# Plain attention layer: tail values as 16 blocks, reciprocals moved behind the first main scores, three bank pairs for the maxima

## The chip, the cores and the metric

The kernel runs on one core of a Trainium2 chip. The metric is the device time of one execution in microseconds (us), lower is better. Three runs of the kernel before gave 2407.03 to 2410.1 us, median 2409.3 us. A core has TensorE (PE, matmuls; PEld its weight loads), VectorE (DVE), ScalarE (ACT), GpSimd (POOL) and SyncE (SP, here the queue that starts all DMA transfers). They run side by side and meet only at semaphores. SBUF is the memory on the core; PSUM is where TensorE writes, in banks of 128 x 512 floats.

## The reference

Two layers run one after the other on x, of shape 2 x 2048 x 512, with 154 context rows per batch:

```
for layer in (0, 1):
    x = x + tanh(g_xattn[layer]) * cross_attention(layernorm(x), ctx_1024)   # 16 heads of 32, 154 keys
    x = x + tanh(g_ffn[layer]) * ffn(layernorm(x))                           # 512 -> 2048 -> 512
```

Layer 0 (the plain layer) has no mask and no norm on q, k and v, and a relu in its ffn. Layer 1 normalises q, k and v, applies a mask, and rounds to a fixed-point grid around a piecewise gelu. Everything is float32.

## The kernel before

Both layers are built by one function, layer_phase, with the flag norm (False for the plain layer). The 4096 rows of x are taken in 8 chunks of 512 (it = 0 to 7). Attention runs over all chunks, then the ffn over all chunks. In the trace the attention of the plain layer takes the stretch from about 65 to 480 us; each chunk from 2 to 6 has the same pattern, about 51 us long. Names in the trace carry prefixes such as l_at_ and l_lay_.

The 16 heads stand in four groups (t = 0 to 3) of four (j = 0 to 3). The 154 keys are split: 128 are the main keys, 26 the tail keys. The tails of the four heads of a group lie in four slots of 32 partitions of p_tail[:, t, :], in the order that group_of(t, j) = (t + j) mod 4 gives. In float32 each matmul is recorded twice; a product of two rounded parts (hi, lo) is three matmuls.

PSUM is six banks named score (the last two of them are also values and sums) and two named bank. Within chunk `it`, TensorE does in this order (the kernel writes the order of every engine out by hand):

- xT_front and neg_front (L1406, L1502): transposes of the next chunk's rows and of the maxima; scores_tail (L1517), 16 blocks of 32 x 32, one for each head, that go to score banks 0 to 3; scores_tail_max (L1526).
- sums_front of the chunk before (L1590).
- q_front for chunk it+1 (L69), group by group, into bank[t % 2]; scores_main (L1546, L1549), which needs the score banks to have been read by the exponentials; values_of (L1563 the tail values, L1567 the main values, L1575 the sums, L1580 the tail sums, at t = 0 only).
- recips of the chunk before (L1609): transposes of the widened reciprocals into bank[0] and bank[1]; DVE multiplies the values by them (c_back, L1019) and ACT and DVE split the product (cT_back L742, lo_of L1036).
- 16 rounds of max_of for chunk it+1 (L1490), which take the pair of score banks 0,1 and 2,3 in turn (round m waits for the reduction of round m-2); from round 2 on a round is followed by three matmuls of y_back, the output projection of chunk it-1.

In the order before, the queue of TensorE in a chunk reads: q_front 0, scores 0, q_front 1, scores 1, values 0, q_front 2 and 3, scores 2, values 1, scores 3, recips 0 and 1, values 2, recips 2 and 3, maxima 0 and 1, values 3, the other maxima with y_back. The tail values are four matmuls with 128 rows and 32 columns (L1563) at the start of every values_of, accumulated in the bank values with the main ones. ACT moves the four results out of that bank (c_evict, L727).

DVE does, per chunk: the low parts of xT (L975), the reciprocals (L1042), q_low 0 and 1 (L983: q32 minus its rounded part, both in SBUF), norm_stats and norm_apply for a later chunk (L934, L943), q_low 2 and 3, c_back, and the 16 reductions (L1012). ACT fills q (q_fill L673), rounds it (q_hi_of L679) and takes the exponentials (L713 tail, L720 main). POOL widens the reciprocals (widen, L543) and adds the gated bias to the residual rows, four rows of 512 per partition in one instruction (add_bias, L534), when the transfer of those rows has landed.

The wait that the change touches most is that of q_front: before, for t >= 2, it is

```
pe.wait_ge(q_row if norm else q_filled, KT * it + t - 1)
if norm and it >= 2:
    pe.wait_ge(c_normed, KT * (it - 2) + t - 1)
```

Of the kernel before, what the change touches and what calls it, by code (L numbers as in the profile page):

```python
# [191 lines left out]
def layer_phase(nc, pre, w, ident, ident_bf, gates, gate, gate_f, norm, place, x_in, front, ahead, src,  # L192
                mid, dst):

    with ExitStack() as ctx:
# [109 lines left out]
        seeded = n.sem("seeded")  # L305
        dve_seeded, act_seeded = n.sem("dve_seeded"), n.sem("act_seeded")
# [304 lines left out]
        def _(act):  # L611
# [110 lines left out]

            def c_evict(it, t):
# [94 lines left out]
            for it in range(NCH):  # L818
                more = it < last
                xT_front(it + 1, (0, 1))  # L820
                neg_front(it)
                xT_front(it + 1, (2, 3))
                exps_tail(it)
                if norm:
                    seed_main(it, 0)
                if it < B:
                    v_tail_of(it)
                if not norm:
                    if more:
                        q_front(it + 1, (0,))  # L830
                    else:
                        relu_hi(0)
                exps_main(it, 0)
                if norm:
                    seed_main(it, 1)
                if not norm:
                    if more:
                        q_front(it + 1, (1,))
                    else:
                        relu_hi(1)  # L840
                exps_main(it, 1)
                if norm:
                    seed_main(it, 2)
                c_evict(it, 0)
                if more and not norm:
                    q_front(it + 1, (2, 3))
                exps_main(it, 2)
                if norm:
                    seed_main(it, 3)
                c_evict(it, 1)  # L850
                if it and norm:
                    cT_back(it - 1, (0, 1))
                exps_main(it, 3)
                if it and not norm:
                    cT_back(it - 1, (0, 1))
                elif not it:
                    front.round_hi(act, "wd")
                c_evict(it, 2)
# [6 lines left out]
                c_evict(it, 3)  # L865
# [63 lines left out]
        def _(dve):  # L929
# [77 lines left out]
            def max_of(it, m):  # L1007
                t, q = m // QT, m % QT
                dve.wait_ge(max_ps, NM * it + m + 1)
                heads = max_banks(it if norm else 0, m).rearrange("p a (h k) -> p a h k", h=2)  # L1010
                to = maxes[:, q, :].rearrange("p (j c) -> p j c", c=DH)[:, :, t]
                nc.vector.tensor_reduce(to, heads, AX.X, ALU.max).then_inc(max_done, 1)  # L1012

            def c_back(it, ts):
                for t in ts:
                    u = KT * it + t
                    c = c_sb[:, it % 2, t, :]
                    dve.wait_ge(rT_ps, u + 1)
                    nc.vector.tensor_tensor(c, c, bank[t % 2][:, :], ALU.mult).then_inc(c_normed, 1)  # L1019
                    if t != ts[0]:  # L1020
                        lo_of(it, t - 1)
                lo_of(it, ts[-1])

            def c_mult(it, ts):
                for t in ts:
                    c = c_sb[:, it % 2, t, :]
                    dve.wait_ge(rT_ps, KT * it + t + 1)
                    nc.vector.tensor_tensor(c, c, bank[t % 2][:, :], ALU.mult).then_inc(c_normed, 1)
# [197 lines left out]
            for it in range(last):  # L1226
# [21 lines left out]
                else:  # L1248
                    q_low(it + 1, (0, 1))
                    norm_stats(it + 2)  # L1250
                    q_low(it + 1, (2, 3))
                    norm_apply(it + 2)
                if it and norm:
                    c_mult(it - 1, (2, 3))
                    c_low(it - 1, (0, 1))
                elif it:
                    c_back(it - 1, (0, 1))
                if norm:
                    norm_apply(it + 2)
                if it and norm:  # L1260
# [20 lines left out]
            for u in range(2):  # L1281
# [3 lines left out]
                else:  # L1285
                    relu_lo(u)
# [7 lines left out]
            else:  # L1294
                c_back(last - 1, (0, 1))
                c_back(last - 1, (2, 3))
            y_back(last - 1, 0)
# [82 lines left out]
        def _(pe):  # L1380
# [56 lines left out]
            def q_front(it, ts):  # L1437
# [30 lines left out]
            def max_of(it, m):  # L1468
# [16 lines left out]
                for a in range(2):  # L1485
                    to = max_banks(it if norm else 0, m)[:, a, :].rearrange("p (h k) -> p h k", h=2)
# [42 lines left out]
            def scores_main(it, t):  # L1529
# [7 lines left out]
                for i, (a, c) in enumerate(((0, 0), (0, 1), (1, 0))):  # L1537
                    for j in range(GH):
                        if i == 0:
                            if not norm:  # L1540
# [10 lines left out]

            def values_of(it, t):
# [6 lines left out]
                if t == 0 and it % CPB == 0:  # L1559
                    pe.wait_ge(v_placed, V_COPIES * (b + 1))  # L1560
                for j in range(GH):
                    own = slice(DH * j, DH * (j + 1))
                    nc.tensor.matmul(values[own, :], keys.v_tail[:, b, t, own], p_tail[:, t, :],  # L1563
                                     start=True, stop=False, skip_group_check=True)
                for j in range(GH):
# [3 lines left out]
                                            p_main[:, t % 2, j, :], start=False, stop=True,  # L1569
# [25 lines left out]
            def recips(it, ts):  # L1595
                for t in ts:
# [5 lines left out]
                    elif t < 2 and it + 2 < NCH:  # L1602
                        pe.wait_ge(q_filled, KT * (it + 2) + t + 3)
                    elif t < 2:
                        pe.wait_ge(y_done, QT * (it - 1) + 3 + t)
                    else:
                        pe.wait_ge(c_normed, KT * it + t - 1)
                    for q in range(QT):
# [81 lines left out]
            for it in range(NCH):  # L1690
# [13 lines left out]
                scores_main(it, 0)  # L1704
                if more:
                    q_front(it + 1, (1,))
                else:
                    first_product(1)
                scores_main(it, 1)
# [3 lines left out]
                if more:  # L1713
                    q_front(it + 1, (2, 3))
                scores_main(it, 2)
                values_of(it, 1)
# [3 lines left out]
                if it and not norm:  # L1720
                    recips(it - 1, (0, 1))
# [144 lines left out]
```

## Time and profile before

| | |
|---|---|
| median of three runs | 2409.3 us |
| profiled execution, its own time | 2409.38 us |
| its span | 2407.6 us |
| TensorE busy | 2352.2 us, 98% |
| VectorE busy | 1504.9 us, 63% |
| ScalarE busy | 1181.1 us, 49% |
| GpSimd busy | 238.6 us, 10% |
| mean granted TensorE clock | 0.991 |

The span is the time from the first to the last recorded instruction; 1.8 us lie around it. Matmuls are pipelined: a matmul of 0.39 us is followed by the next after 0.23 us, so that what a group of matmuls costs is read from the start of one group to the start of the next, not from its duration. Similarly on DVE and ACT the next instruction starts a little before the end of the one before it is recorded.

### The profile page before, as it was taken

What the parts mean: (1) busy time and instruction counts of PE and PEld (TensorE: products, weight loads), DVE (VectorE), ACT (ScalarE), POOL (GpSimd) and SP (SyncE); (2) the same over time, 40 slices, a digit from 0 to 9 for tenths busy, and PEclk for the clock granted to TensorE, in tenths of its full rate; (3) what the DMA queues carried; (4) which work ended last, traced back from release to release, by engine and by line L of the source; (5) the groups of instructions that cost most, each with busy time, mean ns of one, the idle gap of its engine ahead of it and who ended that gap; (6) DMA issues with size and microseconds to landing.
All of it is one profiled execution on the core that took longest, in us unless ns stands there. A gap on an engine that the chain in (4) does not pass through costs nothing.

```text
span 2407.6 us, 32695 instructions
## 1 busy us (share of the span) xinstructions
PE 2352.2 (98%) x12984; PEld 1793.4 (74%) x12984; DVE 1504.9 (63%) x2467; ACT 1181.1 (49%) x1912; POOL 238.6 (10%) x219
## 2 busy tenths in 40 slices
PE   7999999999999999999988999999999999999998
PEld 5566666688888888888765666666788888888886
DVE  5566666442222222223488888886988987988986
ACT  4554434442222222223335666666666666666665
POOL 1021112210000000000111111113000000000000
PEclk9999999999999999999998999999999999999999
DMA  3121112421101101102311111224301001110000
GB/s 130 36 88 53 53 54 80 161 80 53 50 4 53 53 1 53 53 3 86 121 64 50 67 68 67 67 71 145 105 29 43 36 36 36 36 38 33 36 35 19
DMA packets 89159, 140.95 MB, mean 59 GB/s; under 512 B 5040, under 2 KB 27952, under 8 KB 89008
## 3 DMA queue, kind: packets, MB, share of 16 engines
q1 hardware_dynamic: 89008, 138.87, 16.9%
q8 instruction: 103, 1.69, 0.3%
q14 instruction: 48, 0.39, 0.1%
HBM read 105.30 MB, written 33.55 MB: 58 GB/s over the span
## 4 chain that ended last, share of the span: by engine, by line
PE 39%; DVE 8%; ACT 2%; issue 2%; POOL 0%; DVEq 0%; ACTq 0%
PE l_lay_bank L69 19%; PE l_lay_score L69 11%; PE l_lay_score L1490 1%; PE l_lay_score L1546 1%; PE l_lay_score L1563 1%; DVE l_at_at_next L1089 1%; PE l_lay_score L1575 1%; PE l_lay_score L1567 1%; DVE l_at_h_lo L1103 1%; DVE l_at_at_next L1082 1%; PE l_lay_bank L1406 1%; DVE l_at_full L1078 1%; DVE l_at_full L1071 1%; DVE l_at_xTf_lo L975 1%; DVE l_at_maxes L1012 1%
## 5 line engine op out<-in xcount | busy, mean ns | idle before, releaser
L69 PE MATMUL l_lay_score<-l_at_tw_hi,l_at_h_hi 128*128 128x512 f32 x1024 | 401.5, 392 | 5.4 <-DVE l_at_h_lo L1103 4.8
L69 PE MATMUL l_lay_bank<-l_at_xTf_hi,l_at_tw_hi 128*128 128x512 f32 x1024 | 400.0, 391 | 0.0
L69 PE MATMUL l_lay_score<-l_at_tw_hi,l_at_h_lo 128*128 128x512 f32 x1024 | 398.8, 389 | 0.0
L69 PE MATMUL l_lay_bank<-l_at_xTf_hi,l_at_tw_lo 128*128 128x512 f32 x1024 | 398.4, 389 | 0.0
L69 PE MATMUL l_lay_bank<-l_at_xTf_lo,l_at_tw_hi 128*128 128x512 f32 x1024 | 398.4, 389 | 0.0
L69 PE MATMUL l_lay_score<-l_at_tw_lo,l_at_h_hi 128*128 128x512 f32 x1024 | 398.4, 389 | 0.0
L1063 DVE TENSOR_TENSOR l_at_h_lo<-l_at_full,l_at_h_hi 128x512 fp32r<-128x512 f32 x128 | 93.4, 729 | 468.5 <-ACT l_at_h_hi L760 468.5
L755 ACT ACTIVATE l_at_full<-l_lay_bank,l_at_lay_b 128x512 f32<-128x512 f32 x128 | 88.5, 691 | 456.6 <-PE l_lay_bank L69 456.6
L69 PEld LDWEIGHTS l_lay_score<-l_at_tw_hi,l_at_h_hi 128*128 128x128 f32 x1024 | 192.2, 188 | 49.3 <-DVE l_at_h_lo L1103 10.4
L69 PEld LDWEIGHTS l_lay_score<-l_at_tw_hi,l_at_h_lo 128*128 128x128 f32 x1024 | 192.2, 188 | 40.3
L69 PEld LDWEIGHTS l_lay_bank<-l_at_xTf_hi,l_at_tw_hi 128*128 128x128 f32 x1024 | 192.3, 188 | 40.1 <-issue 0.7
L69 PEld LDWEIGHTS l_lay_bank<-l_at_xTf_hi,l_at_tw_lo 128*128 128x128 f32 x1024 | 192.2, 188 | 40.0
L69 PEld LDWEIGHTS l_lay_bank<-l_at_xTf_lo,l_at_tw_hi 128*128 128x128 f32 x1024 | 192.3, 188 | 39.3
L69 PEld LDWEIGHTS l_lay_score<-l_at_tw_lo,l_at_h_hi 128*128 128x128 f32 x1024 | 192.3, 188 | 39.0
L1012 DVE TENSOR_REDUCE l_at_maxes<-l_lay_score 128x4 f32<-128x616 f32 x256 | 197.4, 797 | 27.2 <-PE l_lay_score L1490 24.5
L720 ACT ACTIVATE l_at_p_main<-l_lay_score 128x512 f32<-128x512 f32 x256 | 131.9, 602 | 106.0 <-PE l_lay_score L1549 106.0
L781 ACT ACTIVATE l_at_at_grid<-l_at_at_grid,l_at_lay_grid_bias 128x512 f32<-128x512 f32 x128 | 92.9, 726 | 149.3 <-DVE l_at_at_grid L1093 149.3
L1490 PE MATMUL l_lay_score<-l_at_k_bd,l_at_qT_hi 128*128 128x308 f32 x512 | 130.4, 340 | 6.9 <-ACT l_lay_score L693 3.3
L767 ACT ACTIVATE l_at_grid<-l_at_full,l_at_lay_grid_bias 128x512 f32<-128x512 f32 x128 | 92.4, 722 | 89.5 <-DVE l_at_full L1071 89.5
L1103 DVE SCALAR_TENSOR_TENSOR l_at_h_lo<-l_at_at_grid,l_at_h_hi 128x512 fp32r<-128x512 f32 x128 | 88.1, 688 | 58.2 <-ACT l_at_h_hi L786 58.2
L667 ACT ACTIVATE l_at_xT_hi<-l_lay_bank 128x512 fp32r<-128x512 f32 x64 | 36.6, 597 | 174.7 <-PE l_lay_bank L1406 174.7
L1490 PEld LDWEIGHTS l_lay_score<-l_at_k_bd,l_at_qT_hi 128*128 128x128 f32 x512 | 94.6, 196 | 36.9 <-DVE l_at_maxes L1012 10.0
(196 smaller groups left out, 4063.0 us busy)
## 6 DMA issues: line engine op xcount, KB each, us to landing
both_x_in<-stream SPq DMA_DIRECT2D x25, 1024.0 KB, 5.6
l_at_xg<-stream SPq DMA_DIRECT2D x23, 1024.0 KB, 5.5
stream<-l_at_xg SPq DMA_DIRECT2D x22, 1024.0 KB, 4.3
l_at_tw_raw<-in_l_w SPq DMA_DIRECT2D x64, 256.0 KB, 5.5
both_x_in<-in_x SPq DMA_DIRECT2D x9, 1024.0 KB, 7.8
l_at_xg<-in_x SPq DMA_DIRECT2D x7, 1024.0 KB, 5.5
out<-l_at_xg SPq DMA_DIRECT2D x7, 1024.0 KB, 4.3
l_at_maskT_in<-in_maskT SPq DMA_DIRECT2D x16, 256.0 KB, 3.5
```

The lines of the kernel that those rows point to most:

```text
L69: done = nc.tensor.matmul(out, lhs[a], rhs[b], start=first and n == 0, stop=last and n == len(passes) - 1)
L667: nc.scalar.activation((xT if i < NCH else xTf)[0][:, k, :], (bank if i <= NCH else tr)[k % 2][:, :], ACT.Copy)\
L720: nc.scalar.activation(p_main[:, t % 2, j, :], score[:, j, :], ACT.Exp)\
L755: nc.scalar.activation(full[u % 2][:, :], hid[u % 2][:, :], ACT.Relu, bias=b1[:, u % MT:u % MT + 1]).then_inc(h_full, 1)
L767: nc.scalar.activation(grid[u % 2][:, :], full[u % 2][:, :], ACT.Identity, bias=grid_bias[:, 2:3]).then_inc(gridded, 1)
L781: nc.scalar.activation(at_grid[u % AB][:, :], at_grid[u % AB][:, :], ACT.Identity, bias=grid_bias[:, 3:4]).then_inc(rounded, 1)
L975: nc.vector.tensor_tensor(to[1][:, k, :], ps[k % 2][:, :], to[0][:, k, :].bitcast(F32), ALU.subtract)\
L1012: nc.vector.tensor_reduce(to, heads, AX.X, ALU.max).then_inc(max_done, 1)
L1063: nc.vector.tensor_tensor(h[1][u % HB][:, :], full[u % 2][:, :], h[0][u % HB][:, :].bitcast(F32), ALU.subtract)\
L1071: nc.vector.tensor_scalar(full[u % 2][:, :], hid[u % 2][:, :], b1[:, u % MT:u % MT + 1], ROUND_IN, ALU.add, ALU.add)\
L1103: nc.vector.scalar_tensor_tensor(h[1][u % HB][:, :], at_grid[u % AB][:, :], -ROUND_256, h[0][u % HB][:, :].bitcast(F32), ALU.add, ALU.subt ...
L1490: done = nc.tensor.matmul(to, qT_of(it)[0][:, t, q * P:(q + 1) * P], keys.bd[:, b, t, 2 * a:2 * a + 2, :], start=not norm, stop=True, skip ...
```

## The change

Only the plain layer's order changes, but for one wait that both layers share. Cut to its core:

```diff
@@ TensorE
+            def tail_values(it):
+                pe.wait_ge(exp_done, NS * it + KT)
+                ...
+                for t in range(KT):
+                    for j in range(GH):
+                        c = own_rows[group_of(t, j)]
+                        to = score[own_rows[j], t, :] if t else values[own_rows[j], :]
+                        done = nc.tensor.matmul(to, keys.v_tail[c, b, t, own_rows[j]], p_tail[c, t, :],
+                                                start=True, stop=t > 0, skip_group_check=True)
+                    if t:
+                        done.then_inc(tail_v_ps, 1)
@@ q_front, t >= 2
-                        if norm and it >= 2:
+                        if it >= 2:
                             pe.wait_ge(c_normed, KT * (it - 2) + t - 1)
@@ max_of
+                elif it and m == SEED0:
+                    pe.wait_ge(c_out, KT * it)
+                    pe.wait_ge(s_out, it)
+                elif it and m > SEED0:
+                    pe.wait_ge(max_done, NM * it + pair_before(m) + 1)
-                    to = max_banks(it if norm else 0, m)[:, a, :].rearrange("p (h k) -> p h k", h=2)
+                    to = max_banks(it, m)[:, a, :].rearrange("p (h k) -> p h k", h=2)
@@ scores_main, first pass
-                            if not norm:
+                            if not norm and t == 0 and j == 1:
+                                pe.wait_ge(tail_v_dve, it + 1)
+                            elif not norm and t == 0 and j > 1:
+                                pe.wait_ge(tail_v_act, 2 * it + j - 1)
+                            elif not norm:
@@ y_back
+                if i < KT:
+                    pe.wait_ge(cT_lo, KT * it + i + 1)
                 if i == 0:
-                    pe.wait_ge(cT_lo, KT * it + KT)
+                    pe.wait_ge(c_normed, KT * it + KT)
@@ TensorE, order in a chunk
-                scores_main(it, 0)
+                tail_values(it)
                 q_front(it + 1, (1,))
+                scores_main(it, 0)
+                if it:
+                    recips(it - 1, (0, 1))
+                if more:
+                    q_front(it + 1, (2,))
                 scores_main(it, 1)
                 values_of(it, 0)
-                q_front(it + 1, (2, 3))
                 scores_main(it, 2)
+                q_front(it + 1, (3,))
-                values_of(it, 1)
                 scores_main(it, 3)
-                recips(it - 1, (0, 1))
+                values_of(it, 1)
                 values_of(it, 2)
@@ ACT: two of the tail values are moved to c_sb; only result 0 is evicted
+                    tail_values_out(it, 2)
+                    tail_values_out(it, 3)
@@ DVE
+                    tail_values_out(it, 1)
                     q_low(it + 1, (0, 1))
+                    if it:
+                        c_mult(it - 1, (0, 1))
                     norm_stats(it + 2)
-                    q_low(it + 1, (2, 3))
+                    q_low(it + 1, (2,))
                     norm_apply(it + 2)
+                    q_low(it + 1, (3,))
+                    c_add(it, 1)
                 elif it:
-                    c_back(it - 1, (0, 1))
+                    c_low(it - 1, (0, 1))
+                    c_add(it, 2)
-                    c_back(it - 1, (2, 3))
+                    c_mult(it - 1, (2, 3))
                 for m in range(NM):
                     max_of(it + 1, m)
+                    if m < 2 and it and not norm:
+                        c_low(it - 1, (m + 2,))
+                    if m == 2 and not norm:
+                        c_add(it, 3)
@@ new on DVE
+            def c_add(it, t):
+                c = c_sb[:, it % 2, t, :]
+                if t == 1:
+                    dve.wait_ge(tail_v_dve, it + 1)
+                else:
+                    dve.wait_ge(tail_v_act, 2 * it + t - 1)
+                dve.wait_ge(c_ps, KT * it + t + 1)
+                nc.vector.tensor_tensor(c, values, c, ALU.add).then_inc(c_out, 1)
```

So the tail values of group 0 stay in the bank values and are accumulated with the main ones as before; those of groups 1 to 3 go to score banks 1 to 3, are copied to c_sb, and DVE adds the main values to them later. c_mult is the multiplication of c_back alone, c_low its splitting alone. In rounds 4 to 15 the maxima use a third pair, the banks values and sums. In the last chunk the queue of TensorE has first_product 0 and 1 where the others have q_front 0 and 1, and no q_front 2 and 3.

## Rows read from the trace of the kernel before

**Rows 1.** The page: busy time, and the span in 40 slices of 60.2 us.
```profile
PE 2352.2 (98%) x12984; PEld 1793.4 (74%) x12984; DVE 1504.9 (63%) x2467; ACT 1181.1 (49%) x1912; POOL 238.6 (10%) x219
PE   7999999999999999999988999999999999999998
```

**Rows 2.** Waits of PE from 95 to 480 us: total, times, longest.
```profile
PE l_lay_score L1490 <- DVE l_at_maxes L1012: 2.3, 8, 0.7
PE l_lay_score L1563 <- ACT l_at_c_sb L727: 1.1, 1, 1.1
```

**Rows 3.** Timeline of PE, chunk 5: start us, us, engine, line, instruction, count.
```profile
317.57 1.14 PE L1517 MATMUL l_lay_score<-l_at_q,l_at_k_tail 32*32 32x512 f32 x32
318.64 1.09 PE L1406 MATMUL l_lay_bank<-ident,both_x_in 128*128 128x128 f32 x8
...
321.31 0.50 PE L69 MATMUL l_lay_bank<-l_at_xT_hi,l_front_wq_hi 128*128 128x512 f32 x1
...
324.25 0.50 PE L1546 MATMUL l_lay_score<-l_at_qT_hi,l_at_k_hi 32*128 32x512 f32 x4
...
325.38 0.50 PE L69 MATMUL l_lay_bank<-l_at_xT_hi,l_front_wq_hi 128*128 128x512 f32 x1
...
329.48 1.06 PE L1563 MATMUL l_lay_score<-l_at_p_tail,l_at_v_tail 128*32 128x512 f32 x8
330.36 1.04 PE L1567 MATMUL l_lay_score<-l_at_p_main,l_at_v_main 128*32 128x512 f32 x8
331.22 1.04 PE L1575 MATMUL l_lay_score<-l_at_p_main,l_at_e_main 128*32 128x512 f32 x8
```

**Rows 4.** The same from 347 to 354 us: recips, then two rounds of maxima.
```profile
347.42 1.09 PE L1609 MATMUL l_lay_bank<-ident,l_at_r_wide 128*128 128x128 f32 x8
348.27 0.80 PE L1490 MATMUL l_lay_score<-l_at_k_bd,l_at_qT_hi 128*128 128x308 f32 x4
...
352.80 0.45 PE L1490 MATMUL l_lay_score<-l_at_k_bd,l_at_qT_hi 128*128 128x308 f32 x2
...
353.78 0.45 PE L1490 MATMUL l_lay_score<-l_at_k_bd,l_at_qT_hi 128*128 128x308 f32 x2
```

**Rows 5.** Timeline of DVE, chunk 5: q_low 0 and 1; a c_mult pair of chunk 4.
```profile
325.84 0.69 DVE L983 TENSOR_TENSOR l_at_qT_lo<-l_at_q,l_at_qT_hi 128x512 fp32r<-128x512 f32 x1 [3.79 <-ACT l_at_qT_hi L679]
329.94 1.62 DVE L983 TENSOR_TENSOR l_at_qT_lo<-l_at_q,l_at_qT_hi 128x512 fp32r<-128x512 f32 x1 [3.40 <-ACT l_at_qT_hi L679]
...
293.37 1.28 DVE L1019 TENSOR_TENSOR l_at_c_sb<-l_at_c_sb,l_lay_bank 128x512 f32<-128x512 f32 x2 [1.57 <-PE l_lay_bank L1609]
```

**Rows 6.** Timeline of POOL in the same chunk: add_bias.
```profile
326.33 4.68 POOL L534 TENSOR_TENSOR l_at_xg<-l_at_xg,l_at_gate_bias 128x2048 f32<-128x2048 f32 x1 [3.04 <-DMA l_at_xg<-in_x]
```

**Rows 7.** Chunk 1: q_low 1 on DVE, add_bias on POOL.
```profile
125.84 4.34 DVE L983 TENSOR_TENSOR l_at_qT_lo<-l_at_q,l_at_qT_hi 128x512 fp32r<-128x512 f32 x1 [3.40 <-ACT l_at_qT_hi L679]
125.05 4.58 POOL L534 TENSOR_TENSOR l_at_xg<-l_at_xg,l_at_gate_bias 128x2048 f32<-128x2048 f32 x1 [5.86 <-DMA l_at_xg<-in_x]
```

**Rows 8.** Groups of DVE from 0 to 480 us: busy us, mean ns, idle before.
```profile
L983 DVE TENSOR_TENSOR l_at_qT_lo<-l_at_q,l_at_qT_hi 128x512 fp32r<-128x512 f32 x32 | 33.9, 1059 | 95.6 <-ACT l_at_qT_hi L679 95.6
```

**Rows 9.** Chunk 0: values 3 on PE, the later maxima on PE and DVE.
```profile
97.55 1.06 PE L1563 MATMUL l_lay_score<-l_at_p_tail,l_at_v_tail 128*32 128x512 f32 x8 [1.12 <-ACT l_at_c_sb L727]
100.27 0.84 PE L1490 MATMUL l_lay_score<-l_at_k_bd,l_at_qT_hi 128*128 128x308 f32 x4
100.86 10.67 DVE L1012 TENSOR_REDUCE l_at_maxes<-l_lay_score 128x4 f32<-128x616 f32 x14 [3.15 <-PE l_lay_score L1490]
```

**Rows 10.** Layer 1: two idle stretches of PE before q_front.
```profile
1316.77 0.47 PE L69 MATMUL l_lay_bank<-l_front_wq_hi,l_at_xT_hi 128*128 128x512 f32 x1 [2.30 <-DVE l_at_c_sb L1028]
1538.87 0.47 PE L69 MATMUL l_lay_bank<-l_front_wq_hi,l_at_xT_hi 128*128 128x512 f32 x1 [1.23 <-DVE l_at_c_sb L1028]
```

**Rows 11.** Stretches: length, busy us of PE, PEld, DVE, ACT, POOL, clock, DMA.
```profile
1315.00:1319.00 4.00, 2.23 (x7) 1.84 (x8) 4.00 (x8) 0.00 (x0) 0.76 (x2) 0.83 0.72 209
1319.00:1323.00 4.00, 4.00 (x14) 3.17 (x14) 3.92 (x12) 0.00 (x0) 1.03 (x2) 0.74 0.02 5
```

More of the change, by code:

```diff
@@ L305, in layer_phase @@
         seeded = n.sem("seeded")
+        tail_v_ps, tail_v_dve, tail_v_act = (n.sem(s) for s in ("tail_v_ps", "tail_v_dve", "tail_v_act"))
         dve_seeded, act_seeded = n.sem("dve_seeded"), n.sem("act_seeded")
@@ L721, in exps_main, with tail_values_out @@
                         .then_inc(exp_done, 1)
+            def tail_values_out(it, t):
+                act.wait_ge(tail_v_ps, 3 * it + t)
+                if it >= 2:
+                    act.wait_ge(cT_lo, KT * (it - 2) + t + 1)
+                nc.scalar.activation(c_sb[:, it % 2, t, :], score[:, t, :], ACT.Copy).then_inc(tail_v_act, 1)
             def c_evict(it, t):
@@ L840, in _ @@
                         relu_hi(1)
+                exps_main(it, 0)
+                if norm:
+                    seed_main(it, 1)
+                if more and not norm:
+                    q_front(it + 1, (2,))
                 exps_main(it, 1)
@@ L1017, in c_back @@
                     c = c_sb[:, it % 2, t, :]
+                    if not norm:
+                        dve.wait_ge(c_out, u + 1)
                     dve.wait_ge(rT_ps, u + 1)
@@ L1026, in c_mult @@
                     c = c_sb[:, it % 2, t, :]
+                    if not norm:
+                        dve.wait_ge(c_out, KT * it + t + 1)
                     dve.wait_ge(rT_ps, KT * it + t + 1)
@@ L1284, in _ @@
                     round_hidden(u)
-                else:
-                    relu_lo(u)
+            if not norm:
+                tail_values_out(last, 1)
+                relu_lo(0)
+                relu_lo(1)
+                c_add(last, 1)
             if norm:
@@ L1295, in _ @@
                 c_back(last - 1, (0, 1))
+                c_add(last, 2)
                 c_back(last - 1, (2, 3))
+                c_add(last, 3)
             y_back(last - 1, 0)
@@ L1558, in values_of @@
                     pe.wait_ge(kv_bias, 8)
[L1559 to L1564, printed above, removed]
+                if norm:
+                    if t == 0 and it % CPB == 0:
+                        pe.wait_ge(v_placed, V_COPIES * (b + 1))
+                    for j in range(GH):
+                        own = slice(DH * j, DH * (j + 1))
+                        nc.tensor.matmul(values[own, :], keys.v_tail[:, b, t, own], p_tail[:, t, :],
+                                         start=True, stop=False, skip_group_check=True)
                 for j in range(GH):
@@ L1568, in values_of @@
                                             keys.v_main[:, b, DH * head:DH * (head + 1)],
-                                            p_main[:, t % 2, j, :], start=False, stop=True,
+                                            p_main[:, t % 2, j, :], start=t > 0 and not norm, stop=True,
                                             skip_group_check=True)
@@ L1607, in recips @@
                         pe.wait_ge(c_normed, KT * it + t - 1)
+                        if not norm and it + 2 < NCH:
+                            pe.wait_ge(q_filled, KT * (it + 2) + t + 1)
                     for q in range(QT):
@@ L1708, in _ @@
                     first_product(1)
+                if not norm:
+                    scores_main(it, 0)
+                    if it:
+                        recips(it - 1, (0, 1))
+                    if more:
+                        q_front(it + 1, (2,))
                 scores_main(it, 1)
@@ L1712, in _ @@
                 values_of(it, 0)
-                if more:
+                if more and norm:
                     q_front(it + 1, (2, 3))
                 scores_main(it, 2)
-                values_of(it, 1)
+                if more and not norm:
+                    q_front(it + 1, (3,))
+                else:
+                    values_of(it, 1)
                 if norm and it:
@@ L1719, in _ @@
                 scores_main(it, 3)
-                if it and not norm:
-                    recips(it - 1, (0, 1))
+                if more and not norm:
+                    values_of(it, 1)
                 values_of(it, 2)
```

39 lines of the change are left out of this document (25 added, 14 removed).

## The prediction

> **What bounds the kernel now.** I read the page first, for the shares of the engines and the slices: TensorE is 98% busy, and in the slices of the plain layer's attention (the second to the eighth) it stands at 9 [rows 1]. Then the waits of TensorE for that stretch: from 95 to 480 us it waited 4.1 us in all, of which 2.3 for the reductions of the maxima and 1.1, once, for an eviction [rows 2]. So this stretch is bound by TensorE's own queue: what is taken from that queue is won, and each new wait in it is lost in full, since nothing idle stands behind it. Then I read the timeline of one chunk on each engine (chunk 5, from 315.92 us to 366.93 us, 51.0 us), because the change reorders a chunk, and asked at every step of the new order which wait ends last.
>
> **What the queue of TensorE gains.** The tail values cost 329.48 to 330.36, 0.88 us, four times a chunk: 3.52 us [rows 3]. In their place come 16 blocks of 32 x 32. The nearest row is scores_tail, 16 blocks of the same shape: 317.57 to 318.64, 1.07 us. That gives 2.45 us a chunk. The changes between groups of different shape cost some 0.1 us each; one fewer is left (values 1 and 2 now follow each other) and one more is made (q_front 2 and 3 are parted), and recips followed by q_front cost 0.85 as before maxima [rows 4], not the 1.02 that I read before values. All starts added up, a chunk would take 48.5 us if nothing waited: 2.5 us won.
>
> The price of the 16 blocks is bounded so: below by one pass of 0.86 us as the main values take [rows 3]; above by four passes one after the other, 3.44 us. I take 1.07, as the row of the same shape has it. Trainium skill, "TensorEngine Tiling (Array Packing)", Gotcha 1: PSUM Pressure, says that different row tiles can't use one PSUM bank at the same time. The new blocks do that (the four blocks of a group come from four row tiles and go to one bank). The blocks of scores_tail do it too, and by 1.07 us for all 16 the trace doesn't agree. By that rule it would be the upper bound.
>
> **What it loses, first place: q_front 2 behind c_mult 0.** Now recips 0 and 1 stand before q_front 2 and use the same bank, so q_front 2 waits (c_normed) until DVE has done c_mult 0. On DVE c_mult 0 stands behind q_low 1, and that waits for ACT to fill and round q 1. Let E be the start of scores 0 before (324.25 in chunk 5). TensorE is ready for q_front 2 at E + 1.07 (tail) + 2.94 (q_front 1, as 321.31 to 324.25) + 1.13 (scores, 324.25 to 325.38) + 0.85 = E + 6.0 [rows 3, 4]. DVE starts q_low 1.59 us after the end of a q_front (324.25 to 325.84 [rows 3, 5]), so q_low 1 at E + 5.6; at 0.65 us until the next instruction may start, and 0.64 to 0.68 for c_mult (1.28 for two), c_mult 0 ends at E + 6.93 and TensorE goes on at about E + 6.97. That is 0.95 us of waiting, in chunks 1 to 6: 5.7 us.
>
> But q_low 1 doesn't take 0.69 us here. In chunk 5 it took 1.62 and ended 0.55 us after add_bias on POOL (331.56 against 326.33 + 4.68 = 331.01) [rows 5, 6]; in chunk 1 4.34, again 0.55 us after POOL (130.18 against 129.63) [rows 7]. The group says how much that is over the layer: 32 instructions at 0.69 would be 22.1 us, and they took 33.9 [rows 8]; 11.8 us too many, and by the timelines they lie in six q_low 1, of chunks 1 to 6 (4.34, 2.97, 2.87, 2.23, 1.62 and 1.81 us). Before, norm_stats stood behind q_low 1 and nobody waited for it. Now c_mult 0 does, and TensorE for that. q_low 1 keeps its place (E + 5.6 against E + 5.69 before), and so does add_bias: it starts when its transfer lands, and this hangs on the end of the output projection a chunk earlier, whose distance to the chunk's start is left as it is. So the 11.7 us go into TensorE's wait, with 6 x 0.09 for the earlier start: 5.7 + 11.7 + 0.5 = 17.9 us, from 4.7 us in chunk 1 to 1.9 in chunk 5. If POOL's instruction slid out of the way it would be 5.7; if it slid a us later, 24. I take 17.9. Trainium skill, "SBUF — State Buffer", section SBUF: two separate sides, says that DVE with two SBUF inputs and GpSimd share a port pair as an exclusive lock for the whole instruction. The rows agree: 1.62 and 4.34 against 0.69 us. c_mult has one of its inputs in PSUM, and by that rule runs free; it is what I assumed.
>
> **Second place: maxima round 4.** It writes the banks values and sums, so it waits for c_add 3. DVE does, from the end of c_mult 3 on: maxima 0, c_low 2, maxima 1, c_low 3, maxima 2, c_add 3. At 0.76 us for a reduction (10.67 / 14 [rows 9]) and 0.65 for the others that is 4.2 us. Counted on from recips 2, c_add 3 ends 0.77 us after TensorE is ready for round 4. With 0.12 us before values 2 (c_add 1, behind q_low 3) it is 0.9 us a chunk, 5.3 us for six. After that a round with its y_back takes TensorE 0.98 us [rows 4] and DVE 0.76 plus three y_back: the third pair brings nothing there, and DVE is not the bound. Between 0 and 1.5 us a chunk is possible; I take 0.9.
>
> The other new waits end early: tail values out on ACT (0.62 us each) are done about 1.2 us before scores 0; exponentials 3, now behind values 1 in the queue, end 0.5 us before maxima 0; the widening on POOL is done some 6 us ahead. If one of these covers went, it would cost its difference alone.
>
> **Chunk 0** has no recips, so not the first wait. The wait of 1.12 us before values 3 goes (c_add 2 isn't behind the rounding of wd), and the tail gain comes: round 2 of the maxima starts at about 97.1 instead of 100.27 [rows 9]. From there DVE is the bound, 14 reductions in 10.67 us, and c_add 3 is added (0.65): 3.1 - 0.65 = 2.5 us won. A third bank pair helps nothing where DVE has no gap. **Chunk 7** has no q_front 2, so scores 1 comes right behind recips and waits for exponentials 0, some 1.4 us; 2.5 - 1.4 = 1.1 us won. The wait of y_back on cT_lo, now split, was no wait before in either layer: nothing, and the rest of layer 1 keeps its order.
>
> **Sum without the clock.** Chunks 1 to 6: 6 x 2.5 = 15.0 won, 17.9 + 5.3 = 23.2 lost: 8.2 us slower. Chunks 0 and 7: 3.6 us faster. Together 4.6 us slower, 2414.0 against the profiled execution's 2409.38, which lies 0.1 us above the median.
>
> **The clock.** After 2.30 us idle before 1316.77 the granted clock went to 0.83 and 0.74 over the next two stretches of 4 us [rows 10, 11], which is a while at 1.2 instead of 2.4 GHz: 0.17 x 4 + 0.26 x 4 = 1.7 us lost. After 1.23 us idle before 1538.87 it stayed at 1.00 in the windows there. The new waits are 4.7, 3.3, 3.2, 2.5, 1.9 and 2.1 us in chunks 1 to 6. I count a fall for the four that are longer than 2.30: 4 x 1.7 = 6.8 us, bounds 0 and 6 x 1.7 = 10.2. That makes 2420.7; for the part of a fall that lies inside the idle time I take off 1: 2419.7.
>
> **The rivals.**
> A. *The long wait doesn't come*: POOL's add_bias moves off, or q_low 1 gets in before it. For it: the landing times of the transfer varied by some 1.5 us between the chunks. Against: all six were hit before, and POOL's 4.6 us cover E + 5.6 in each. Then 5.7 instead of 17.9 and no clock loss: 2409.4 - 15.0 - 3.6 + 5.7 + 5.3 = 2401.8. This is the case on the other side: TensorE's 2.5 us a chunk decide as soon as the new waits stay under them. Chance 0.14.
> B. *The wait comes, the clock stays*: the idle stretches fall so that the clock isn't taken back. For it: 1.23 us left it alone. Against: 2.30 didn't. 2414. Chance 0.22.
> C. *The 16 blocks are done in four passes*, by the page's rule: 2.4 us more a chunk. Part of it hides in the first wait, which then ends at the same time: about 19 us more, less 11 hidden: some 2422 with B's clock, as there the waits are short. Against it stands scores_tail. Chance 0.05.
> D. My forecast: the wait and the clock, 2419.7. Chance 0.59.
>
> **How the numbers follow.** From no change a measurement of this kernel can tell about 0.2%, 4.8 us. A is faster. B at 2414 lies on the edge of 0.2% (2414.1) and goes half to same, half to slower; of D a tenth may end within 0.2%, if two falls alone come. Faster 0.13, same 0.17, slower 0.70. The range reaches from 2404, which leaves out A's lower part, to 2428, which takes in 24 us instead of 17.9 and two more falls; without A the range would be 2411 to 2428.
>
> **What would show it.** In the profile after: L1517's and the new tail group's starts 1.07 us apart from the next group; q_front (L69) idle before it, released by DVE's c_mult, 1.9 to 4.7 us in six chunks, with q_low 1 still at 1.6 to 4.4 us; maxima (L1490) waiting 0.8 us for DVE at round 4; a clock below 1.00 in the slices from 110 to 400 us; chunks of 51.3 us and more. I am wrong if q_front's wait is about 1 us or names another engine, if a chunk takes under 51 us, or if the tail group takes over 3 us.

## The result, and the profile after

The changed kernel takes 2416.66 us (median of eight runs, 2415.03 to 2420.12), the kernel before 2409.45 us beside it (eight runs, 2403.57 to 2411.72). The ratio is 1.0035, 95% interval 1.0026 to 1.0044: slower by 7.2 us or 0.35%. The forecast was 2419.7 us. The profiled execution took 2417.11 us, 7.7 us more than that of before.

The page of the changed kernel first: TensorE's busy time has fallen by 9.3 us and the span has grown by 7.7, so its idle time has grown by 17.0 us. The busy time is not all work: it holds what the falls of the clock below add to the matmuls.

```profile
span 2415.3 us, 32800 instructions
PE 2342.9 (97%) x12984; PEld 1789.8 (74%) x12984; DVE 1521.0 (63%) x2499; ACT 1174.5 (49%) x1904; POOL 240.3 (10%) x219
```

The waits of TensorE from 60 to 490 us (total, times, longest). The first three are new beside [rows 2]. In the first, by far the largest, q_front waits for c_mult; in the other two round 4 of the maxima waits (the third row is chunk 0, where it waits for c_add 3).

```profile
PE l_lay_bank L69 <- DVE l_at_c_sb L1057: 15.9, 6, 4.3
PE l_lay_score L1540 <- issue: 2.5, 6, 0.4
PE l_lay_score L1540 <- DVE l_at_c_sb L1037: 1.3, 1, 1.3
PE l_lay_score L1540 <- DVE l_at_maxes L1022: 1.2, 6, 0.3
```

The timeline of TensorE shows where: the first matmul of q_front 2 in chunks 1 to 6.

```profile
128.83 0.77 PE L69 MATMUL l_lay_bank<-l_at_xT_hi,l_front_wq_hi 128*128 128x512 f32 x1 [4.31 <-DVE l_at_c_sb L1057]
...
183.99 0.47 PE L69 MATMUL l_lay_bank<-l_at_xT_hi,l_front_wq_hi 128*128 128x512 f32 x1 [3.32 <-DVE l_at_c_sb L1057]
...
237.29 0.47 PE L69 MATMUL l_lay_bank<-l_at_xT_hi,l_front_wq_hi 128*128 128x512 f32 x1 [1.98 <-DVE l_at_c_sb L1057]
...
289.18 0.47 PE L69 MATMUL l_lay_bank<-l_at_xT_hi,l_front_wq_hi 128*128 128x512 f32 x1 [2.16 <-DVE l_at_c_sb L1057]
...
342.47 0.47 PE L69 MATMUL l_lay_bank<-l_at_xT_hi,l_front_wq_hi 128*128 128x512 f32 x1 [1.99 <-DVE l_at_c_sb L1057]
...
394.33 0.47 PE L69 MATMUL l_lay_bank<-l_at_xT_hi,l_front_wq_hi 128*128 128x512 f32 x1 [2.13 <-DVE l_at_c_sb L1057]
```

What DVE and POOL did in chunk 5 answers to [rows 5, 6]: q_low 1 takes 1.88 us and ends 0.54 us after add_bias (341.72 against 341.18), and c_mult stands right behind it.

```profile
339.84 1.88 DVE L993 TENSOR_TENSOR l_at_qT_lo<-l_at_q,l_at_qT_hi 128x512 fp32r<-128x512 f32 x1 [3.11 <-ACT l_at_qT_hi L680]
341.65 1.27 DVE L1057 TENSOR_TENSOR l_at_c_sb<-l_at_c_sb,l_lay_bank 128x512 f32<-128x512 f32 x2
...
336.31 4.87 POOL L535 TENSOR_TENSOR l_at_xg<-l_at_xg,l_at_gate_bias 128x2048 f32<-128x2048 f32 x1 [3.07 <-DMA l_at_xg<-in_x]
```

The granted clock around six of these waits (columns as in [rows 11]; the clock stands behind POOL's column):

```profile
126.00:130.00 4.00, 1.17 (x3) 1.01 (x4) 4.00 (x5) 0.00 (x0) 1.53 (x1) 0.56 0.00 0
130.00:134.00 4.00, 4.00 (x15) 2.87 (x17) 2.04 (x8) 0.06 (x1) 1.76 (x4) 0.58 0.00 0
184.00:188.00 4.00, 4.00 (x11) 3.17 (x12) 3.20 (x10) 0.00 (x0) 0.60 (x2) 0.57 0.00 0
...
236.00:240.00 4.00, 2.71 (x12) 2.17 (x12) 4.00 (x7) 0.58 (x2) 0.00 (x0) 1.00 0.00 0
...
290.00:294.00 4.00, 4.00 (x18) 2.68 (x20) 2.39 (x9) 0.30 (x1) 1.41 (x3) 0.57 0.00 0
342.00:346.00 4.00, 3.53 (x24) 2.70 (x28) 3.68 (x11) 0.49 (x1) 0.20 (x1) 1.00 0.00 0
394.00:398.00 4.00, 3.67 (x24) 2.86 (x28) 3.54 (x11) 0.65 (x1) 0.26 (x2) 1.00 0.00 0
```

The clock was at 1.2 GHz for a while behind the waits of 4.31, 3.32 and 2.16 us (in the first it fell before the wait was over) and stayed at 2.4 GHz behind 1.98, 1.99 and 2.13 us.

From one start of neg_front to the next, the chunks took, in us:

```
chunk        0      1      2      3      4      5      6      sum
before   46.04  51.67  51.04  51.03  51.02  51.01  51.05   352.86
after    43.08  57.81  54.63  51.74  53.42  51.76  51.84   364.28
change   -2.96  +6.14  +3.59  +0.71  +2.40  +0.75  +0.79   +11.42
```

From chunk 7's neg_front on, the execution is 3.8 us shorter (1985.4 against 1989.2 us). Of this, 0.5 lie in chunk 7, the remainder behind it, where the two programs are nearly alike.

### The profile page after: what moved, and what is told of

Read it like the earlier page. It is cut to its first block, busy times and chain, and to the rows that moved or that the text cites. A ratio compares the mean times of both kernels' runs of the same rounds, so it can differ in the third digit from the quotient of the medians.

```text
span 2415.3 us, 32800 instructions
## 1 busy us (share of the span) xinstructions
PE 2342.9 (97%) x12984; PEld 1789.8 (74%) x12984; DVE 1521.0 (63%) x2499; ACT 1174.5 (49%) x1904; POOL 240.3 (10%) x219
## 4 chain that ended last, share of the span: by engine, by line
PE 38%; DVE 8%; ACT 2%; issue 2%; POOL 0%; DVEq 0%; ACTq 0%
PE l_lay_bank L69 19%; PE l_lay_score L69 11%; PE l_lay_score L1540 1%; PE l_lay_score L1600 1%; PE l_lay_score L1636 1%; DVE l_at_at_next L1118 1%; PE l_lay_score L1648 1%; PE l_lay_score L1640 1%; DVE l_at_h_lo L1132 1%; DVE l_at_at_next L1111 1%; DVE l_at_full L1107 1%; DVE l_at_full L1100 1%; PE l_lay_bank L1451 1%; DVE l_at_xTf_lo L985 1%; DVE l_at_maxes L1022 1%
## 5 line engine op out<-in xcount | busy, mean ns | idle before, releaser
L1540 PEld LDWEIGHTS l_lay_score<-l_at_k_bd,l_at_qT_hi 128*128 128x128 f32 x512 | 93.3, 194 | 41.1 <-issue 11.5
```

The costliest lines, as they stand in the source:

```text
L1540: done = nc.tensor.matmul(to, qT_of(it)[0][:, t, q * P:(q + 1) * P], keys.bd[:, b, t, 2 * a:2 * a + 2, :], start=not norm, stop=True, skip ...
```

## The experiments

Each is an edit of the changed kernel and was timed in five rounds beside the kernel before. All medians:

```
kernel               median us (lowest to highest, runs)   before    ratio [95% interval]
the change           2416.66 (2415.03 to 2420.12, 8)       2409.45   1.0035 [1.0026, 1.0044]
e1_mult_first        2401.21 (2398.69 to 2402.51, 6)       2408.73   0.9965 [0.9953, 0.9977]
e3_short_bias        2403.55 (2399.45 to 2404.37, 8)       2408.73   0.9978 [0.9968, 0.9988]
e4_recips_back       2402.35 (2399.13 to 2404.93, 6)       2408.73   0.9973 [0.9962, 0.9985]
e5_two_pairs         2415.13 (2410.01 to 2418.39, 7)       2408.73   1.0026 [1.0015, 1.0037]
e2_mult_add          2396.81 (2394.34 to 2401.54, 6)       2409.09   0.9955 [0.9941, 0.9968]
e6_late_recips       2393.94 (2392.64 to 2395.64, 5)       2409.09   0.9941 [0.9929, 0.9952]
e7_filled_wait       2414.69 (2412.97 to 2416.16, 8)       2409.09   1.0025 [1.0015, 1.0035]
```

The theory: q_front 2 waits for c_mult 0, which is late because q_low 1 stands ahead of it and is held by add_bias; the clock's falls come on top. The rivals: that the 16 blocks or the other moved steps cost the time, that the place of recips is at fault whatever DVE's order is, and that the clock is the larger part.

### e1_mult_first: c_mult ahead of q_low 1

```diff
-                    q_low(it + 1, (0, 1))
+                    q_low(it + 1, (0,))
                     if it:
                         c_mult(it - 1, (0, 1))
+                    q_low(it + 1, (1,))
```

> The changed kernel with one edit on DVE: c_mult 0 and 1 stand ahead of q_low 1 instead of behind it. My theory (q_front 2 waits for c_mult 0, and that for q_low 1, which POOL's add_bias stretches): the wait before q_front 2 falls from 15.9 us in six chunks to about 0.5 us each, 3 in all, the three falls of the clock go too (some 4 us), and the time is near 2416.7 - 13 - 4 = 2400. Rival 1 (the loss is in what the blocks and the shape changes cost TensorE, or in DVE's added work as such): DVE does the same work in another order, so nothing over 2 us moves, 2415 to 2417. Rival 2 (c_mult itself is stretched by POOL, or waits for the transposes): the wait keeps most of its length, 2412 to 2416.

2401.21 us. One instruction moved on DVE turns 0.35% slower into 0.35% faster. The waits of TensorE:

```profile
PE l_lay_bank L69 <- DVE l_at_c_sb L1057: 3.0, 6, 0.5
PE l_lay_score L1541 <- issue: 2.4, 6, 0.4
PE l_lay_score L1541 <- DVE l_at_c_sb L1037: 1.3, 1, 1.3
```

q_front 2 waits 3.0 us in all instead of 15.9, and chunks 2 to 6 take 50.2 to 50.3 us (but 51.7 in chunk 1). In chunk 5, c_mult starts while POOL is at add_bias, and q_low 1 comes when that is over and takes 0.68 us:

```profile
324.76 1.28 DVE L1057 TENSOR_TENSOR l_at_c_sb<-l_at_c_sb,l_lay_bank 128x512 f32<-128x512 f32 x2 [3.42 <-PE l_lay_bank L1685]
325.96 0.68 DVE L993 TENSOR_TENSOR l_at_qT_lo<-l_at_q,l_at_qT_hi 128x512 fp32r<-128x512 f32 x1
...
321.13 4.66 POOL L535 TENSOR_TENSOR l_at_xg<-l_at_xg,l_at_gate_bias 128x2048 f32<-128x2048 f32 x1 [3.25 <-DMA l_at_xg<-in_x]
```

c_mult takes its usual 0.64 us each: one of its inputs lies in PSUM, and it isn't held. In chunk 1 both lie wholly inside add_bias (123.76 to 125.04 us, against 122.54 to 127.13) and take 1.28 us together as well. The forecast had assumed this, and the rule of the Trainium skill, "SBUF — State Buffer", section SBUF: two separate sides, which names two SBUF inputs, agrees with it. The 16 blocks and the place of recips are unchanged here, so they are not what made the change slow.

### e3_short_bias: POOL's instruction shortened

The kernel leaves out most of the output bias of the plain layer.

```diff
+                if not norm and i < last:
+                    nc.gpsimd.tensor_tensor(to[:, 0, 0:8], to[:, 0, 0:8], rows[:, 0:8], ALU.add)\
+                        .then_inc(xg_done, 1)
+                    return
```

> The changed kernel, but POOL's add_bias in the plain layer's attention, for chunks 0 to 6, adds only 8 columns of one row in place of 4 x 512 (most of the output bias is left out). My theory: q_low 1 falls from 1.9 to 4.2 us to 0.69 in all chunks, and the wait before q_front 2 to about 0.95 us each, 5.7 in all: 10 us less, and with the falls of the clock 2416.7 - 10 - 4 = 2402 to 2404. Rival (q_low 1 is long for another reason, such as the timing of ACT's rounding or a transfer into SBUF): q_low 1 and the wait stay, 2415 to 2417.

2403.55 us. Groups of DVE from 0 to 480 us (busy us, mean ns, idle before), the changed kernel and then this one:

```profile
L993 DVE TENSOR_TENSOR l_at_qT_lo<-l_at_q,l_at_qT_hi 128x512 fp32r<-128x512 f32 x32 | 33.2, 1037 | 84.6 <-ACT l_at_qT_hi L680 84.6
```

```profile
L997 DVE TENSOR_TENSOR l_at_qT_lo<-l_at_q,l_at_qT_hi 128x512 fp32r<-128x512 f32 x32 | 22.1, 690 | 75.3 <-ACT l_at_qT_hi L684 75.3
```

All 32 q_low now take 0.68 to 0.69 us, and nothing on DVE was changed. The wait of q_front 2 in this kernel:

```profile
PE l_lay_bank L69 <- DVE l_at_c_sb L1061: 4.8, 6, 0.8
```

So 11.1 of the 15.9 us were POOL's instruction, as the excess of the group over 22.1 us (33.2 less 22.1 = 11.1) says by itself; the other 4.8 us, 0.8 a chunk, are the order on DVE.

### e4_recips_back: reciprocals 0 and 1 behind scores 3 again

The waits of the old order come back with it: q_front 2 of the plain layer no longer waits for c_normed, recips 0 and 1 wait until ACT has filled q 2 and 3, and in chunk 7 ACT does its part of splitting products 0 and 1 behind the last exponentials.

```diff
@@ TensorE
                     scores_main(it, 0)
-                    if it:
-                        recips(it - 1, (0, 1))
...
                 scores_main(it, 3)
+                if it and not norm:
+                    recips(it - 1, (0, 1))
                 if more and not norm:
                     values_of(it, 1)
@@ DVE
-                    if it:
-                        c_mult(it - 1, (0, 1))
...
                     q_low(it + 1, (3,))
+                    if it:
+                        c_mult(it - 1, (0, 1))
```

> The changed kernel with one part undone: recips 0 and 1 go back behind scores 3 (now ahead of values 1), DVE's c_mult 0 and 1 behind q_low 3, q_front 2 has no wait on c_normed in the plain layer; the 16 blocks and the three bank pairs stay. My theory: no wait of q_front; what is left per chunk is TensorE's own queue, 2.5 us shorter than before, less 0.4 at round 4 of the maxima: 2409.4 - 6 x 2.0 - 4 = 2393 to 2396. Rival 1 (the 16 blocks bring less than they seem to): 2405 to 2410. Rival 2 (the values' sum on DVE holds up values 2 or the maxima when c_mult stands beside it): 2398 to 2404, with waits of L1640 or L1540 for L1037.

2402.35 us, above what was expected. The wait of q_front is gone and chunks 2 to 6 take 49.7 to 49.8 us. Two terms had been set too low. The maxima's round 4 still waits for c_add 3 (below). And from chunk 7's neg_front to the chunk's own recips 1 it took 45.15 us, against 42.29 before and 41.85 in e1. With no recips behind scores 0, TensorE idles 1.11 us before the exponentials of group 0 are done, and then works at 1.2 GHz for a while: the granted clock was 0.83 in the 10 us from 420 on. Values 3 of that chunk also wait 0.6 us for c_add 2. The timeline of TensorE, then that stretch:

```profile
420.02 1.87 PE L1602 MATMUL l_lay_score<-l_at_qT_hi,l_at_k_hi 32*128 32x512 f32 x4 [1.11 <-ACT l_at_p_main L721]
```

```profile
420.00:430.00 10.00, 9.98 (x75) 3.49 (x75) 2.46 (x2) 5.89 (x12) 6.17 (x2) 0.83 0.01 2
```

### e5_two_pairs: the maxima back on two bank pairs

```diff
-                elif it and m == SEED0:
-                    pe.wait_ge(c_out, KT * it)
-                    pe.wait_ge(s_out, it)
-                elif it and m > SEED0:
-                    pe.wait_ge(max_done, NM * it + pair_before(m) + 1)
...
-                    to = max_banks(it, m)[:, a, :].rearrange("p (h k) -> p h k", h=2)
+                    to = max_banks(it if norm else 0, m)[:, a, :].rearrange("p (h k) -> p h k", h=2)
```

> The changed kernel with one part undone: the maxima of the plain layer take two bank pairs in turn in all rounds. My theory (the third pair brings nothing where TensorE is the bound, and costs the wait of round 4 for c_add 3): the waits of 0.4 us before round 4 in six chunks and 1.25 in chunk 0 go, 2416.7 - 2.5 - 0 to 1 = 2413 to 2415. Rival (the third pair decouples TensorE from DVE, which has more to do in these rounds now): waits of L1540 for L1022 appear in rounds 3 to 6, and the time is 2418 to 2422.

2415.13 us, 1.5 below the change; the intervals overlap, so the sign isn't sure. The trace shows two parts that nearly cancel. In chunk 5 of the changed kernel the rounds 3 and 4 start 1.55 us apart where the period is 0.98:

```profile
362.89 0.45 PE L1540 MATMUL l_lay_score<-l_at_k_bd,l_at_qT_hi 128*128 128x308 f32 x2
...
364.44 0.52 PE L1540 MATMUL l_lay_score<-l_at_k_bd,l_at_qT_hi 128*128 128x308 f32 x2 [0.40 <-issue]
```

With two pairs the same two rounds start 1.00 us apart, and the rounds 4 and 5 1.21 us, for the reduction behind c_add 3. So of the 0.57 us before round 4 some 0.2 come back a round later, and chunk 5 takes 51.39 us against 51.76:

```profile
362.79 0.45 PE L1535 MATMUL l_lay_score<-l_at_k_bd,l_at_qT_hi 128*128 128x308 f32 x2
363.79 0.52 PE L1535 MATMUL l_lay_score<-l_at_k_bd,l_at_qT_hi 128*128 128x308 f32 x2
365.00 0.55 PE L1535 MATMUL l_lay_score<-l_at_k_bd,l_at_qT_hi 128*128 128x308 f32 x2
```

In chunk 0, where DVE bounds the maxima, the third pair did help: neg_front of chunk 1 starts at 108.70 in the changed kernel and at 110.21 here. The wait on c_add 3 is the third pair's price, and the forecast's sentence that the pair helps nothing in chunk 0 was wrong. The 1.5 us are not the pair's alone, though: here the clock was at 0.50 in most of these rounds (0.73 from 102 to 104 us, 0.50 from 104 to 110), in the changed kernel from 106 us on. With three pairs such a clock cost nothing: in e1, at 0.50 from 102 to 110 us, chunk 0 took 43.11 us, the same as at full clock in e7. With the clock full for most of these rounds the pair is worth some 0.6 us: the 14 reductions from round 2 on took DVE 10.67 us before [rows 9], and 10.63 us with c_add 3 among them in the changed kernel (98.01 to 108.64).

### e2_mult_add: e1, and c_add 3 two places earlier

```diff
-                    if m < 2 and it and not norm:
-                        c_low(it - 1, (m + 2,))
-                    if m == 2 and not norm:
+                    if m in (0, 2) and it and not norm:
+                        c_low(it - 1, (2 + m // 2,))
+                    if m == 1 and not norm:
                         c_add(it, 3)
```

> e1_mult_first with one more edit on DVE: c_add 3 stands behind reduction 1 of the maxima instead of 2, and c_low 3 behind reduction 2. My theory (round 4 of the maxima waits for c_add 3, at 0.6 us a chunk as the starts of rounds 4 and 5 show, 1.3 in chunk 0): the gap between the starts of rounds 3 and 4 falls from 1.55 to 1.0 us, 4 us less in all, 2396 to 2398. Rival (round 4 waits for something else, as the profile puts it down to no releaser): 1.55 us stays, 2400 to 2402.

2396.81 us, 12.3 below its own runs of the kernel before, where e1 was 7.5 below its own: 4.8 us more. The chunk goes from 50.25 to 49.6 us; chunks 1 to 6 save 3.4 us together and chunk 0 another 0.6. The wait under "issue" that stood before round 4 is gone:

```profile
PE l_lay_bank L69 <- DVE l_at_c_sb L1057: 3.0, 6, 0.5
PE l_lay_score L1541 <- DVE l_at_maxes L1022: 1.4, 8, 0.2
```

### e6_late_recips: both waits removed

e4 in chunks 1 to 6, the changed kernel's order in chunk 7, and e2's order of c_add 3.

```diff
@@ TensorE
-                    if it:
+                    if not more:
                         recips(it - 1, (0, 1))
...
                 scores_main(it, 3)
+                if it and more and not norm:
+                    recips(it - 1, (0, 1))
```

> e4_recips_back, but in chunk 7 recips 0 and 1 stand right behind scores 0 as in the changed kernel, and c_add 3 stands behind reduction 1 as in e2_mult_add. In e4 a chunk took 49.8 us against 51.0 before, but chunk 7 took 2.9 us more than before, with a wait of 1.1 us for the exponentials and a fall of the clock. My theory: that was chunk 7's own wait; now a chunk takes 49.2 us, chunk 7 about what it took in e1_mult_first, and the time is 2393 to 2396. Rival (late recips cost by themselves, c_mult beside c_add holds up values 2): 2398 to 2402.

2393.94 us, ratio 0.9941: by the medians 15.2 us faster than the kernel before and 22.7 faster than the change. It beats both. All waits of TensorE from 60 to 490 us:

```profile
PE l_lay_score L1540 <- DVE l_at_maxes L1022: 0.7, 4, 0.2
PE l_lay_bank L69 <- DVE l_at_xT_lo L985: 0.6, 1, 0.6
PE l_lay_bank L1684 <- DVE l_at_xg L1081: 0.5, 1, 0.5
PE l_lay_score L1552 <- DVE l_at_maxes L1022: 0.4, 1, 0.4
PE l_lay_score L1540 <- ACT l_at_p_main L721: 0.2, 1, 0.2
```

A chunk takes 49.1 us. One gap is left that the list doesn't hold: values 2 starts 1.18 us after the sums of group 1 instead of 0.86, behind c_add 1.

```profile
332.05 1.04 PE L1648 MATMUL l_lay_score<-l_at_p_main,l_at_e_main 128*32 128x512 f32 x8
333.23 1.06 PE L1640 MATMUL l_lay_score<-l_at_p_main,l_at_v_main 128*32 128x512 f32 x8
```

The remainder can be read group by group, from start to start. Against the chunk of before (51.0 us): 3.52 us of tail values gone, the blocks 1.07, q_front 2 and 3 parted 0.27 (5.65 us together before, 2 x 2.96 apart), the gap before values 2 0.3. That gives 49.1.

### e7_filled_wait: TensorE kept busy through the wait

```diff
                         recips(it - 1, (0, 1))
+                    if it and more:
+                        pe.wait_ge(recip_done, it)
+                        for _ in range({1: 38, 2: 28}.get(it, 16)):
+                            nc.tensor.transpose(sums[:, 0:P], ident[:, :], ident[:, :])
```

> The changed kernel with transposes of the identity, 128 x 128, into the bank sums (free at that point) put between recips 1 and q_front 2: 38 in chunk 1, 28 in chunk 2, 16 in chunks 3 to 6, about 4.1, 3.0 and 1.7 us, so that TensorE works through its wait for c_mult 0. The wait itself isn't shortened. My theory (the lost time is the wait, 15.9 us, and on top of it falls of the clock behind it, three in the profiled run at about 1.5 us): the falls go, 2411 to 2413. Rival 1 (the clock does not matter here): 2416 to 2418. Rival 2 (all of the loss is the clock): below 2405.

2414.69 us, above what was expected: 2.0 us below the change, and the intervals overlap, so even the sign isn't sure. In chunk 1 the wait is filled and the clock stays at 1.00 behind it:

```profile
123.30 4.31 PE L1796 MATMUL l_lay_score<-ident 128*128 128x128 f32 x38
127.77 0.47 PE L69 MATMUL l_lay_bank<-l_at_xT_hi,l_front_wq_hi 128*128 128x512 f32 x1 [0.16 <-DVE l_at_c_sb L1057]
...
128.00:132.00 4.00, 4.00 (x32) 2.75 (x35) 2.97 (x10) 1.16 (x2) 0.83 (x2) 1.00 0.02 4
```

Chunk 1 takes 54.7 us instead of 57.8, and chunks 0 to 5 together 306.6 instead of 312.4, 5.9 us less. This is not the falls alone. In chunk 1 the clock had been low before the wait, too (0.75 and 0.50 in the two stretches of 4 us from 104 on), and here it was at 1.00 there, though the edit does nothing before that point. And q_low 1, which POOL stretches, took 2.30 us in chunk 2 and 2.74 in chunk 3, where it had taken 3.22 and 1.88. Chunk 4, where q_low 1 took as long as before (2.02 against 2.06 us), shows a fall by itself: 51.86 against 53.42 us, 1.6 us.

In the profiled runs most of these 5.9 us are gone at the end: from chunk 7's neg_front on it took 1990.5 us here and 1985.4 in the changed kernel, though the programs are nearly alike there. The traces show where. From 490 to 1160 us and from 1340 to 2400 us the clock is at 1.00 in both. Between them, in layer 1, it falls several times, and here more than in the changed kernel; q_front also waits longer there. The stretch and the wait of TensorE behind 480 us, the changed kernel first, then this one:

```profile
1160.00:1340.00 180.00, 163.87 (x1010) 112.51 (x1008) 129.01 (x229) 81.77 (x150) 32.30 (x47) 0.94 0.24 78
PE l_lay_bank L69 <- DVE l_at_c_sb L1057: 2.3, 3, 1.1
```

```profile
1160.00:1340.00 180.00, 162.00 (x992) 110.87 (x990) 132.11 (x231) 81.06 (x149) 32.33 (x47) 0.92 0.23 77
PE l_lay_bank L69 <- DVE l_at_c_sb L1057: 4.2, 3, 2.4
```

0.02 of clock over 180 us are 3.6 us (an estimate from two rounded numbers), and the wait is 1.9 us longer: together about the 5.1 us. Over all nine profiled runs the time from chunk 7 on goes with that clock: 1986.4 us at 0.95 (e2), 1985.4 to 1988.2 at 0.94 (four runs), 1988.9 and 1989.2 at 0.93, 1990.5 and 1994.7 at 0.92 (the last is e4, which lost 2.9 us in chunk 7). Why the clock falls there more often in one run than in another isn't shown.

## Why the prediction was right

It was right in sign and mechanism, and near in size (2419.7 against 2416.66, with the profiled run at 2417.11). Two of its sums are 0.1 us off by their own terms (2414.0 + 6.8 is 2420.8, and the new wait of chunk 5 comes to 2.0 us); nothing hangs on it. Case D came in: the wait and the falls of the clock. A needed the long wait to stay away, B the clock to stay up; neither happened. Step by step, for chunks 1 to 6:

- **The 16 blocks.** Forecast 1.07 us. In chunk 5 the group and the q_front 1 behind it take 4.01 us, and q_front alone 2.94. Right; case C is out. The rule of the Trainium skill, "TensorEngine Tiling (Array Packing)", Gotcha 1: PSUM Pressure, that different row tiles can't use one PSUM bank at the same time, doesn't show as a price here: 1.07 us, where four passes would take 3.44.

```profile
334.25 1.14 PE L1619 MATMUL l_lay_score<-l_at_p_tail,l_at_v_tail 32*32 32x512 f32 x32
...
338.26 0.51 PE L1600 MATMUL l_lay_score<-l_at_qT_hi,l_at_k_hi 32*128 32x512 f32 x4
```

- **q_front 2 behind c_mult 0.** Forecast 17.9 us. The list of waits says 15.9, but it counts from the recorded end of recips (339.39 + 1.09 = 340.48 in chunk 5), and the forecast from where the next group could start (339.39 + 0.85). That is 0.24 us more a time: 17.3 us. Both halves hold: the order on DVE cost 4.8 + 6 x 0.24 = 6.2 (e3; forecast 5.7 + 0.5), and POOL 11.1 (forecast 11.7). The second is less for "add_bias keeps its place", which held in chunk 5 (10.0 us behind neg_front's start, as before) but not in chunk 3: 9.9 us behind it (231.08 - 221.14), 11.3 before (225.62 - 214.30), and q_low 1 of chunk 3 took 1.88 us, where it had taken 2.87 before.
- **The chunk without waits.** Forecast 48.5 us. Chunk 5 took 51.76; less 2.23 and 0.87 (next point) that is 48.7. The term that was too small is the parting of q_front 2 and 3, 0.27 us and not some 0.1.
- **c_add.** Forecast 0.77 before round 4 and 0.12 before values 2, 0.9 in sum. Measured 0.57 (1.55 less 0.98) and 0.30: 0.87. The sum is right, its split not.
- **Chunk 0 and chunk 7.** Forecast 2.5 and 1.1 us won; measured 3.0 and 0.5. In chunk 0 the third pair helped after all (e5). In chunk 7 the wait for the exponentials of group 0 came as described (2.50 us from scores 1 to values 0, where 1.13 is usual), and scores 3 was held up too (1.55 us instead of 1.13).
- **The clock.** Forecast four falls of 1.7 us, less 1: 5.8. There were three; in chunk 3, where a fourth was counted, the wait was short for the reason above. That 2.30 us parts the waits with a fall from those without was not borne out: 2.16 us in chunk 4 had one. Two cost 1.7 us (0.43 x 4) each; in the one of chunk 1, q_front 2 took 5.01 us instead of 2.96, 2.05 lost. That is 5.5 us in place. In the whole program, filling the waits gave back 2.0 us in the median, not clear of the noise (e7).
- **The layers behind.** The forecast had no term for them. Chunks 0 to 6 were to be 11.5 us longer (8.2 + 5.8 - 2.5) and were 11.4. Everything from chunk 7 on was to be 1.1 shorter and was 3.8. The forecast lies 2.7 us too high for this alone. The traces show most of it in layer 1: from 1160 to 1340 us the mean clock was 0.94 against 0.93 before, which is 1.8 us (an estimate, as above), and behind 480 us q_front waited 2.3 us against 3.5. The forecast had no reason to expect it, and e7 shows how it can go the other way.

The sum for chunks 1 to 6 is then 6 x 48.7 = 292.2, plus 17.3, 5.2 and 5.5: 320.2 us. Measured were 321.2. Chunk 1 alone is 1.6 us above its own sum (57.81 against 48.7 + 4.55 + 0.87 + 2.05). Its clock was low before the wait too, as in the kernel before (there 51.67 us for a chunk that otherwise takes 51.0); but 0.6 us of extra time come at full clock as well (e4: 50.36 us against 49.8), where its transposes wait 0.7 us for DVE's low part of xT. That the sum to chunk 6 hit 11.4 us within 0.1 is luck in part: the chunk without waits was set 1.0 us too low over six chunks, the wait 0.6 too high, the clock 0.3 too high and chunk 0's gain 0.5 too low.

## What to carry to other kernels

When a step is moved ahead of a wait, walk back through the queue of the engine that releases it: the instruction that decided here was neither moved nor on any path before, and was slow only because of a third engine. An instruction whose recorded duration varies (0.69 to 4.34 us for one shape) is a wait in disguise; give it a place where nobody stands behind it. A saving and a loss of like size can come in one change: parted by experiment, this one holds 15 us of gain against the kernel before (e6).

## What the runs showed of the hardware

- DVE's subtraction with both inputs in SBUF is held until POOL's 128 x 2048 addition is over, and ends 0.5 us after it; its multiplication with one input in PSUM runs beside that addition at its usual 0.64 us (e1).
- The length of an idle stretch alone doesn't tell whether the clock falls: behind 2.16 us it did, behind 2.13 us it didn't, and with TensorE busy on transposes in the same place it never did from 117 to 400 us (e7). Nor does the same work always bring the same falls: at the end of chunk 0, where these kernels are alike, the clock was at 0.50 from 102 to 110 us in e1, and at 1.00 in e4 and e7.
- A fall from 2.4 to 1.2 GHz cost 1.7 us of TensorE's time in place (0.43 x 4, chunks 2 and 4). In nine profiled runs the mean clock of one stretch of 180 us in layer 1 lay between 0.92 and 0.95, and the runs with less of it took longer behind the plain layer's attention (e7).
- A wait can stand in the list under "issue" and vanish when a DVE instruction is moved (round 4, e2). The list of waits is short of some, too: 0.3 us before values 2 showed only in the starts.
